# The last sixteen images' modes are turned ahead of the coefficient spread instead of behind the low modes

## The chip, the cores and the metric

One core of one Trainium2 chip runs the whole kernel. The metric is the device time of one execution in microseconds (us). The times shown are the median, lowest and highest of three runs; the profile is of one more execution.

## The reference

The input is x with 4 batches, 64 images each, 256x256 float32. Every batch is normalized in 32 groups of columns (`_gn`), and then goes through a spectral attention block. Cut to what matters:

```python
xa_n = _inorm(xa)                                   # every image by its own mean and variance
k, q = _spec_conv(xa_n, kw, (64, 64)), _spec_conv(xa_n, qw, (64, 64))   # 16 x 8 low modes
v    = _spec_conv(xa_n, vw, (256, 256))
att  = softmax(q @ k.T * sqrt(64*64)) @ v           # 64 x 64, over the images of a batch
att  = _inorm(att) + xa
mix  = _spec_conv(_inorm(att), mix_w, (256, 256), bias=mix_bias)        # 64 x 32 modes
out  = _inorm(_inorm(mix + skip)) + att
return x + out
```

`_spec_conv` is a 2D real Fourier transform, a product of each kept mode with a complex weight, and the inverse transform.

## The kernel before

All 64 images of a batch lie in SBUF at once, in X, and their half transformed modes in Y. The kernel works batch by batch, and each batch has two parts. `attend(b)` is the middle of the computation: statistics, low modes, attention among the images, mixing of all modes, and the coefficients with which each image is put together. `produce(b, more)` then makes the output images four by four (quad u), and while there is a next batch it also loads that batch's images into the places that come free, transforms them forward and sums their squares.

Each engine has a program of its own, in an order written out by hand; they meet through counting semaphores. An engine that waits holds up everything behind it in its program. The steps that matter here:

- `raw_modes(b, m, ...)` on TensorE (PE, line 404) transforms sixteen images (m of 0 to 3) along the width. `keep_raw(b, m)` on ScalarE (ACT, L608) copies them to SBUF and gives `raw_kept`.
- `turn_modes(b, m)` on PE (L418) turns the sixteen images' modes into the layout of the mixer, 8 matmuls that the trace shows as 16 records, in two groups of eight images; it gives `modes_made`. Group g (0 to 7) is then squared by ACT (`mode_powers`, L612), weighted by VectorE (DVE, `weigh_modes`, L909), and treated by GpSimd (POOL, `weigh` L833 and `add_products` L838). Groups 6 and 7 come from `turn_modes(b, 3)`.
- `energy(b, part)` on PE (L455) is a one-column matmul that sums the energies. From it DVE makes a variance (`deviations`), ACT a root (`root`, L651), and DVE the coefficients (`coefficients`, L1133 on, the last of it a memset at L1142), giving `coef_made`. Part 0 is for the first images, part 1 for the others, later in `produce`.
- `spread(b, part)` on PE (L460, L461) brings the coefficients to the partitions. `keep_spread` on DVE copies them: BIA and SCL for the images' synthesis, and C2 (L1155), from which POOL makes the factors ALPHA (`alphas`, L846; ACT adds one, L647) and scales the images X (`scale_x`, L855).
- `turn_low(b, part)` on PE (L472, 32 small matmuls, 64 records) makes the low modes' share D; DVE adds it (`add_low`, L909, Y<-Y,psB), and ACT turns the low piece (`low_piece`, L617 and L618), which gives `s_ready`.
- `inverse_h(b, q)` on PE (L433) is the inverse along the height for quad q. `keep_t` on ACT (L630) copies it, `inverse_w` on PE (L448) is the inverse along the width, `finish` on DVE (L909, X<-X,ps) adds it to the scaled image, and the sync queue stores it (L313) and loads the next batch's images in its place (L309). `forward` on PE (L386) is their forward transform.
- In the last batch ACT also writes factors for some images that DVE scales itself (`vector_alphas`, L640).

`coefficients` of part 0 works for about 2 us while `energy` has been issued and PE has nothing to do; ACT then runs `root(b, 0)`, `mode_powers(b, 5)` and `keep_raw(b, 3)` in this order.

Of the kernel before, what the change touches and what calls it, by code (L numbers as in the profile page):

```python
# [82 lines left out]
def spectral_block(nc, x, mix_re, mix_im, mix_mirror, low_w, low_mix, scalars,  # L83
# [8 lines left out]
    with ctx:  # L92
# [181 lines left out]
        def coef_bank(b, part):  # L274
            return second_bank(b) if part else psT[1]
# [20 lines left out]
        def over(ap, dims):  # L296

            return bass.AP(ap.tensor, ap.offset, [list(ap.ap[0])] + dims)
# [76 lines left out]
        def _(pe):  # L375
# [23 lines left out]
            def raw_modes(b, m, steps):  # L399

                for step in steps:
                    c, k = step // 2, step % 2
                    for t in range(2):
                        last = mm(psR[m % 2][64 * t:64 * t + 64, :], GWR[:, c, k, :, :].rearrange("p r v -> p (r v)"),  # L404
                                  Y[:, c, k, 16 * m + 8 * t:16 * m + 8 * t + 8, :],
                                  start=step == 0, stop=step == 3)
                    if step == 3:
                        last.then_inc(raw_made, 1)

            def turn_modes(b, m):  # L410

                if m:
                    pe.wait_ge(mode_weighted, 8 * b + 2 * m - 1)
                pe.wait_ge(raw_kept, 4 * b + m + 1)
                for pair in range(4):
                    for t in range(2):
                        rows = slice(64 * t, 64 * t + 64)
                        last = mm(over(psM[(2 * m + t) % 3][:, 64 * pair:64 * pair + 1], [[256, 2], [1, 64]]),  # L418
                                  raw_of(m)[rows, 128 * pair:128 * pair + 128], TURN[rows, :], start=True, stop=True)
                        if pair == 3:  # L420
                            last.then_inc(modes_made, 1)

            def inverse_h(b, q):

                for n, (q0, q1) in enumerate(PIECES):
                    if q == q0:
                        pe.wait_ge(s_ready, 3 * b + n + 1)
                if q:
                    pe.wait_ge(t_kept, 32 * b + 2 * q)
                for part in range(2):  # L430
                    for h in range(2):
                        rows = slice(64 * h, 64 * (h + 1))
                        last = mm(psT[h][:, 0:H],  # L433
                                  S[rows, q, part, :, :].rearrange("p j n -> p (j n)"),
                                  INVH[rows, part, :], start=part == 0, stop=part == 1)
                last.then_inc(t_made, 1)
# [16 lines left out]
            def energy(b, part):  # L453
                pe.wait_ge(energy_part, 10 * b + (6, 10)[part])
                mm(coef_bank(b, part)[0:IMGS, 496:497], FPH, ONES[:, 0:1],  # L455
                   start=True, stop=True).then_inc(energy_sum, 1)

            def spread(b, part):
                pe.wait_ge(coef_made, 2 * b + part + 1)
                mm(coef_bank(b, part)[:, 320:416], SIDE[:, :], RC, start=True, stop=True)  # L460
                mm(coef_bank(b, part)[:, 416:480], ONES[0:IMGS, :], E2, start=True, stop=True).then_inc(coef_spread, 1)  # L461

            def turn_low(b, part):

                j0, j1 = (0, 4 * SPLIT) if part == 0 else (4 * SPLIT, 32)
                pe.wait_ge(d_made, 2 * b + part + 1)
                for r in range(2):
                    for v in range(LV):
                        vals = D[:, r, :].rearrange("p (u v) -> p u v", v=LV)[:, :, v]
                        col = LV * r + v  # L470
                        for h in range(2):
                            last = mm(low_bank(b, part)[64 * h:64 * h + LU, col:16 * (j1 - j0):16], vals, EI[:, 2 * j0 + h:2 * j1:2],  # L472
                                      start=True, stop=True)
                last.then_inc(d_turned, 1)

            def warm(n):
                for _ in range(n):
                    mm(psZ[0][:, 0:256], ONES[:, :], FWD[:, :, :].rearrange("p a n -> p (a n)"), start=True, stop=True)

            def attend(b):  # L480

                warm(WARM[0])
                pe.wait_ge(totals_in, b + 1)
                mm(psTot[:, 0:64], ONES[:, :], TOT, start=True, stop=True).then_inc(totals_made, 1)
                for c in range(WC):
                    mm(psSta[0:IMGS, 16 * c:16 * (c + 1)], Y[:, c, 0, :, U0], GROUP[:, :], start=True, stop=True)
                pe.wait_ge(pad_made, b + 1)
                mm(psSta[0:IMGS, 32:64], PAD, SEL[:, :], start=True, stop=True).then_inc(sums_made, 1)
                warm(WARM[1])

                pe.wait_ge(scaled_w, 4 * b + 2)
                for c in range(WC):
                    for k in range(2):
                        last = mm(psZ[0][64 * k:64 * k + 64, :], GWR[:, c, k, :, :].rearrange("p r v -> p (r v)"),  # L494
                                  Y[:, c, k, :, U0 + 1:U0 + 9], start=c == 0, stop=c == WC - 1)
                last.then_inc(z_raw, 1)
                pe.wait_ge(scaled_w, 4 * b + 4)
                for c in range(WC):
                    last = mm(psZ[1][0:64, 0:IMGS], GWR[:, c, 0, :, :].rearrange("p r v -> p (r v)"),
                              Y[:, c, 0, :, U0], start=c == 0, stop=c == WC - 1)  # L500
                last.then_inc(z_raw, 1)
                raw_modes(b, 0, (0,))

                pe.wait_ge(z_kept, 2 * b + 2)
                for n in range(8):
                    mm(psZ[2][0:IMGS, 32 * n:32 * (n + 1)], ZT[:, 64 * n:64 * (n + 1)], MIRROR[:, :],
                       start=True, stop=True)
                mm(psZ[2][0:IMGS, 256:272], ZT0, MIRROR[0:64, 0:16], start=True, stop=True).then_inc(z_made, 1)
                raw_modes(b, 0, (1, 2, 3))
                raw_modes(b, 1, (0,))  # L510

                pe.wait_ge(qk_ready, b + 1)
                for n in range(8):
                    o, size = (72, 64) if n // 4 else (0, 72)
                    src = QKV[:, (n % 4) // 2, n % 2, o:o + size]
                    last = nc.tensor.transpose(psQ[0:size, 64 * n:64 * (n + 1)], src, EYE[:, :])
                last.then_inc(qk_turned, 1)
                turn_modes(b, 0)
                pe.wait_ge(qk_kept, 2 * b + 2)
                for n in range(4):  # L520
                    size, q, k = ((72, n, 2 + n), (64, 2 + n, 4 + n))[n // 2]
                    last = mm(psB[0:IMGS, 256:320], QT[0:size, q, :], QT[0:size, k, :], start=n == 0, stop=n == 3)
                last.then_inc(logits_made, 1)
                raw_modes(b, 1, (1, 2, 3))

                pe.wait_ge(probs_made, b + 1)
                nc.tensor.transpose(psB[0:IMGS, 320:384], PR[:, 0, :], EYE[:, :]).then_inc(probs_turned, 1)
                turn_modes(b, 1)
                pe.wait_ge(probs_kept, b + 1)
                mm(psA[0:IMGS, 0:2 * LOW], PR[:, 1, :], QKV[:, 2, :, :].rearrange("p r n -> p (r n)"),  # L530
                   start=True, stop=True).then_inc(att_made, 1)
                raw_modes(b, 2, (0, 1, 2, 3))
                raw_modes(b, 3, (0,))
                turn_modes(b, 2)
                raw_modes(b, 3, (1, 2, 3))
                energy(b, 0)
                spread(b, 0)
                turn_low(b, 0)
                turn_modes(b, 3)
                inverse_h(b, 0)  # L540

            def produce(b, more):
# [43 lines left out]
            for b in range(B):  # L586
                attend(b)
                produce(b, b < B - 1)
# [669 lines left out]
```

## Time and profile before

| | us |
|---|---|
| median of 3 runs (lowest to highest) | 636.29 (633.12 to 636.81) |
| profiled execution | 633.88 |
| its span in the trace | 632.1 |
| PE, DVE, ACT, POOL busy | 581.8, 482.8, 356.6, 336.4 |
| mean granted clock of PE | 0.961 |

The profiled execution is 1.8 us longer than its span, and 2.4 us shorter than the median. Times in the trace count from the span's start. A record's busy time of PE is modelled at its end, so where two records follow each other, the starts are what is read. The granted clock is a share of full speed: 1.00 is 2.4 GHz, 0.50 is 1.2 GHz.

### The profile page before, as it was taken

The page shows a single profiled execution, that of the slowest core. Times are in us where ns is not written, and L with a number is a line of the kernel's source. Part 1 is how long each engine was busy: PE and PEld are TensorE (multiplying, and loading weights), DVE is VectorE, ACT ScalarE, POOL GpSimd, SP SyncE. Part 2 cuts the span into 40 slices and gives each one's busy share as a digit, 9 for nine tenths or more (in the row PEclk, how much of TensorE's full clock was granted, in tenths as well). Part 3 has the DMA queues.
Part 4 walks back from the last instruction along what each step waited for, and adds up shares of the span by engine and source line. Part 5 has one row for each costly group of instructions (what it writes and reads, how often), then busy time and mean ns, then how long its engine had stood idle before and what let it go on. Part 6 is the DMA issues. An engine that isn't in the chain of part 4 may idle for free.

```text
span 632.1 us, 13832 instructions
## 1 busy us (share of the span) xinstructions
PE 581.8 (92%) x5072; PEld 480.6 (76%) x5072; DVE 482.8 (76%) x1095; ACT 356.6 (56%) x778; POOL 336.4 (53%) x398
## 2 busy tenths in 40 slices
PE   9999996999999996999999999699999999866994
PEld 9999644899899842789999874488999985354773
DVE  4666787787776888688777768777877768878996
ACT  6888353575666534466666635256576662543431
POOL 0270046959960014896975002597897200479993
PEclk9999996999999999899999999789999999979998
DMA  8993003899899901579999950279799993005787
GB/s 318 326 385 110 1 2 96 293 311 301 292 313 322 328 14 41 208 264 305 287 332 309 317 206 1 67 255 303 252 334 322 322 303 112 0 34 192 263 309 270
DMA packets 75522, 142.55 MB, mean 226 GB/s; under 512 B 6016, under 2 KB 6656, under 8 KB 75456
## 3 DMA queue, kind: packets, MB, share of 16 engines
q1 hardware_dynamic: 75456, 141.67, 65.6%
q8 instruction: 41, 0.67, 0.5%
q14 instruction: 25, 0.20, 0.1%
HBM read 74.54 MB, written 67.11 MB: 224 GB/s over the span
## 4 chain that ended last, share of the span: by engine, by line
PE 53%; DVE 25%; ACT 7%; POOL 5%; DMA 5%; issue 5%; SPq 0%; DVEq 0%; ACTq 0%; POOLq 0%
PE psY L386 23%; PE psP L448 15%; PE psT L433 7%; DVE QP L945 6%; DVE X L909 4%; ACT SQ L604 3%; POOL X L855 3%; DMA X<-in_x 3%; DVE Y L909 3%; DVE SQ L909 3%; DMA out<-X 2%; PE psP L494 1%; DVE IM L913 1%; DVE SQ L919 1%; DVE IM L916 1%
## 5 line engine op out<-in xcount | busy, mean ns | idle before, releaser
L855 POOL TENSOR_TENSOR X<-X,ALPHA 128x512 f32<-128x512 f32 x244 | 254.6, 1080 | 31.7 <-DVE IM L1142 18.5
L386 PE MATMUL psY<-FWD,X 128*128 128x128 f32 x1856 | 224.0, 279 | 2.3 <-DMA X<-in_x 2.2
L386 PEld LDWEIGHTS psY<-FWD,X 128*128 128x128 f32 x1856 | 213.1, 193 | 15.5 <-issue 13.9
L945 DVE TENSOR_REDUCE QP<-SQ 128x32 f32<-128x512 f32 x256 | 162.2, 680 | 48.3 <-ACT SQ L604 48.1
L909 DVE TENSOR_TENSOR X<-X,psP 128x512 f32<-128x512 f32 x192 | 125.8, 684 | 51.2 <-PE psP L448 23.9
L448 PE MATMUL psP<-INVW,T 64*128 64x256 f32 x768 | 141.9, 404 | 13.4 <-DVE X L909 7.8
L604 ACT ACTIVATE SQ<-X 128x512 f32<-128x512 f32 x232 | 132.4, 621 | 9.1 <-DVE Y L916 6.4
L833 POOL TENSOR_TENSOR Y<-Y,OMEGA 128x256 f32<-128x256 f32 x32 | 24.5, 765 | 189.0 <-ACT Y L612 189.0
L448 PEld LDWEIGHTS psP<-INVW,T 64*128 64x128 f32 x768 | 93.8, 191 | 34.2 <-ACT T L630 14.8
L630 ACT ACTIVATE T<-psT,BIA,SCL 128x256 f32<-128x256 f32 x128 | 65.3, 560 | 94.3 <-PE psT L433 89.8
L596 ACT ACTIVATE Y<-psY 128x512 f32<-128x512 f32 x128 | 76.2, 595 | 46.5 <-PE psY L386 45.3
L433 PE MATMUL psT<-INVH,Y 64*128 64x256 f32 x512 | 72.4, 402 | 0.0
L448 PE MATMUL psB<-INVW,T 64*128 64x256 f32 x256 | 68.9, 390 | 0.0
L433 PEld LDWEIGHTS psT<-INVH,Y 64*128 64x128 f32 x512 | 54.9, 203 | 5.2
L448 PEld LDWEIGHTS psB<-INVW,T 64*128 64x128 f32 x256 | 46.7, 190 | 0.0
L909 DVE TENSOR_TENSOR X<-X,psB 128x512 f32<-128x512 f32 x64 | 43.6, 682 | 1.8 <-POOL X L855 1.3
L838 POOL TENSOR_TENSOR Y<-Y 128x256 f32<-128x256 f32 x32 | 24.1, 754 | 19.7 <-DVE Y L909 19.4
L404 PE MATMUL psT<-Y,GWR 128*64 128x512 f32 x128 | 30.8, 600 | 0.0
L404 PE MATMUL psP<-Y,GWR 128*64 128x512 f32 x128 | 30.6, 598 | 0.0
L647 ACT ACTIVATE ALPHA<-ALPHA,ONES 128x256 f32<-128x256 f32 x32 | 16.2, 505 | 24.0 <-POOL ALPHA L846 24.0
L846 POOL TENSOR_TENSOR ALPHA<-MR,C 128x256 f32<-128x256 f32 x32 | 19.7, 616 | 15.0 <-DVE C L1155 11.3
L617 ACT ACTIVATE Y<-Y 128x128 f32<-128x128 f32 (+2 forms) x44 | 12.9, 293 | 23.4 <-POOL Y L838 16.6
(206 smaller groups left out, 552.5 us busy)
## 6 DMA issues: line engine op xcount, KB each, us to landing
X<-in_x SPq DMA_DIRECT2D x116, 512.0 KB, 5.4
out<-X SPq DMA_DIRECT2D x116, 512.0 KB, 3.9
X<-in_x SPq DMA_DIRECT2D x24, 256.0 KB, 4.2
Y<-in_x SPq DMA_DIRECT2D x6, 1024.0 KB, 5.1
out<-X SPq DMA_DIRECT2D x24, 256.0 KB, 3.8
INVH<-t_inv_h SPq DMA_DIRECT2D x1, 256.0 KB, 8.8
LW<-in_low_w SPq DMA_DIRECT2D x1, 204.0 KB, 5.7
FWD<-t_fwd SPq DMA_DIRECT2D x1, 128.0 KB, 2.1
```

The costliest lines, as they stand in the source:

```text
L386: last = mm(psY[p % 2][:, (2 * i + c) * 128:(2 * i + c + 1) * 128], image(nb, 2 * p + i)[:, a, c * 128:(c + 1) * 128], FWD[:, a, :], start ...
L404: last = mm(psR[m % 2][64 * t:64 * t + 64, :], GWR[:, c, k, :, :].rearrange("p r v -> p (r v)"), Y[:, c, k, 16 * m + 8 * t:16 * m + 8 * t ...
L433: last = mm(psT[h][:, 0:H], S[rows, q, part, :, :].rearrange("p j n -> p (j n)"), INVH[rows, part, :], start=part == 0, stop=part == 1)
L448: last = mm(out_bank(b, 2 * s + i)[:, W * a:W * (a + 1)], T[rows, s % 4, 128 * a:128 * (a + 1)], INVW[rows, :], start=True, stop=True)
L596: nc.scalar.activation(Y[:, :, :, i0:i0 + 3:2, :].rearrange("p c k i u -> p i (c k) u"), psY[p % 2][:, :].rearrange("p (i n u) -> p i n u" ...
L604: nc.scalar.activation(SQ[:, n % RING, :], flat_image(nb, n), ACT.Square).then_inc(squared, 1)
L630: nc.scalar.activation(T[:, p % 4, :], psT[p % 2][:, 0:H], ACT.Identity, bias=BIA[:, p:p + 1], scale=SCL[:, p:p + 1]).then_inc(t_kept, 1)
L833: P.tensor_tensor(v, v, over(OMEGA[:, 0:1], [[0, 4], [0, 2], [1, NV]]), MUL).then_inc(powers_weighted, 1)
L838: P.tensor_tensor(S[:, 2 * g:2 * g + 2, 0, :, :].rearrange("p q j n -> p q (j n)"), w[:, 0, :].rearrange("p (q n) -> p q n", q=2), w[:, 1, ...
L855: P.tensor_tensor(v, v, al, MUL).then_inc(x_scaled, 1)
L909: return V.tensor_tensor(out, a, b, op)
L945: V.tensor_reduce(QP[:, 4 * (k % 2) + place(n) % 4, :], SQ[:, n % RING, :].rearrange("p (a g j) -> p g a j", a=HC, j=GW), AX.XY, ADD).then ...
```

## The change

In `attend` of TensorE, `turn_modes(b, 3)` moves from behind `turn_low(b, 0)` to a place behind `energy(b, 0)`, ahead of `spread(b, 0)`. Nothing else is changed, on no other engine.

```diff
                 turn_modes(b, 2)
                 raw_modes(b, 3, (1, 2, 3))
                 energy(b, 0)
+                turn_modes(b, 3)
                 spread(b, 0)
                 turn_low(b, 0)
-                turn_modes(b, 3)
                 inverse_h(b, 0)
```

On TensorE, in each of the four batches, the difference of the two orders is this one, with what each row waits for; L418 is the turn, L460 and L461 the spread, L472 the low modes, L433 `inverse_h`:

```order
 L455 MATMUL psT<-ONES,Y 64x1 [waits energy_part]
+L418 MATMUL psY<-TURN,Y 128x2x64 [waits raw_kept,mode_weighted]
+L418 MATMUL psY<-TURN,Y 128x2x64 x7
 L460 MATMUL psT<-Y,SIDE 128x96 [waits coef_made]
 L461 MATMUL psT<-Y,ONES 128x64
 L472 MATMUL psB<-Y 17x20 [waits d_made]
 L472 MATMUL psB<-Y 17x20 x31
-L418 MATMUL psY<-TURN,Y 128x2x64 [waits raw_kept,mode_weighted]
-L418 MATMUL psY<-TURN,Y 128x2x64 x7
 L433 MATMUL psT<-INVH,Y 128x256 [waits s_ready]
```

The eight matmuls now stand ahead of the coefficients' spread, and `inverse_h` directly behind the low modes. On ScalarE the same stretch is the same before and now; it gives `raw_kept` (the L608 row, for which the moved step waits) and it has a group that the moved step makes (the L612 row behind the low piece):

```order
L651 ACTIVATE IM<-IM 64x1 [waits var_made]
L612 ACTIVATE Y<-psP 128x256 [waits modes_made]
L608 ACTIVATE Y<-psP 128x512 [waits raw_made]
L647 ACTIVATE ALPHA<-ALPHA,ONES 128x256 [waits alpha_made]
L617 ACTIVATE Y<-Y 128x2x2x8 [waits d_added]
L618 ACTIVATE Y<-Y 128x2x2x8
L612 ACTIVATE Y<-psY 128x256 [waits modes_made]
L630 ACTIVATE T<-psT,BIA,SCL 128x256 [waits t_made,scl_kept]
```

Nothing moved on this engine.

## Rows read from the trace of the kernel before

**Rows 1.** The page, busy us (share of the span) and instructions.
```profile
PE 581.8 (92%) x5072; PEld 480.6 (76%) x5072; DVE 482.8 (76%) x1095; ACT 356.6 (56%) x778; POOL 336.4 (53%) x398
```
**Rows 2.** Chain of waits, first batch: start us, us, what.
```profile
101.71 1.24 PE psB L472 x64
102.95 2.01 PE psY L418 x16
104.95 1.73 PE psT L433 x8
```
**Rows 3.** Timeline, first batch: start us, us, engine, line, [idle before <-releaser].
```profile
97.56 0.28 PE L455 MATMUL psT<-ONES,Y 128*64 128x1 f32 x2 [2.44 <-DVE Y L909]
98.73 0.58 ACT L608 ACTIVATE Y<-psP 128x512 f32<-128x512 f32 x1
100.59 0.74 PE L460 MATMUL psT<-Y,SIDE 64*128 64x96 f32 x2 [2.76 <-DVE IM L1142]
102.99 1.35 DVE L909 TENSOR_TENSOR Y<-Y,psB 17x64 f32<-17x64 f32 x4
103.64 0.21 ACT L618 ACTIVATE Y<-Y 128x32 f32<-128x32 f32 x1
117.94 3.84 PE L386 MATMUL psY<-FWD,Y 128*128 128x128 f32 x32
```
**Rows 4.** Chain of waits, last batch.
```profile
559.00 0.58 POOL ALPHA L846
573.74 1.28 ACT psY L640 x4
```
**Rows 5.** Timeline of TensorE, an earlier turn in the first batch.
```profile
79.73 1.11 PE L418 MATMUL psY<-TURN,Y 64*128 64x128 f32 x15
```
**Rows 6.** Windows: us, busy of PE, PEld, DVE, ACT, POOL, PEclk, DMA share, GB/s.
```profile
98.00:98.50 0.50, 0.00 (x0) 0.00 (x0) 0.46 (x3) 0.14 (x2) 0.00 (x0) 0.68 0.07 16
111.50:112.00 0.50, 0.50 (x6) 0.41 (x4) 0.00 (x0) 0.50 (x2) 0.50 (x2) 0.67 1.04 401
...
251.50:252.00 0.50, 0.00 (x0) 0.00 (x0) 0.46 (x4) 0.00 (x0) 0.07 (x1) 0.78 0.93 356
258.50:259.00 0.50, 0.10 (x2) 0.00 (x0) 0.00 (x0) 0.29 (x1) 0.50 (x1) 0.89 0.00 0
...
401.50:402.00 0.50, 0.22 (x2) 0.13 (x2) 0.21 (x1) 0.35 (x2) 0.00 (x0) 0.97 0.00 0
...
555.50:556.00 0.50, 0.00 (x0) 0.00 (x0) 0.50 (x3) 0.36 (x1) 0.50 (x1) 0.57 0.00 0
562.00:562.50 0.50, 0.50 (x6) 0.37 (x4) 0.50 (x1) 0.00 (x0) 0.50 (x1) 0.61 0.00 0
```
**Rows 7.** Timeline, last batch.
```profile
555.28 0.58 ACT L608 ACTIVATE Y<-psP 128x512 f32<-128x512 f32 x1
557.13 0.74 PE L460 MATMUL psT<-Y,SIDE 64*128 64x96 f32 x2 [2.75 <-DVE IM L1142]
```
**Rows 8.** Timeline of TensorE, second and third batch.
```profile
249.50 0.28 PE L455 MATMUL psT<-ONES,Y 128*64 128x1 f32 x2 [2.46 <-DVE Y L909]
252.53 0.74 PE L460 MATMUL psT<-Y,SIDE 64*128 64x96 f32 x2 [2.75 <-DVE IM L1142]
...
268.30 3.84 PE L386 MATMUL psY<-FWD,Y 128*128 128x128 f32 x32
...
401.44 0.28 PE L455 MATMUL psT<-ONES,Y 128*64 128x1 f32 x2 [2.44 <-DVE Y L909]
```
**Rows 9.** Chain of waits, ends of the first and second batch.
```profile
207.02 4.95 DMA X<-in_x
...
352.51 5.69 DMA out<-X
358.22 5.42 DMA X<-in_x
```
**Rows 10.** Timeline of VectorE, last batch.
```profile
573.75 0.69 DVE L909 TENSOR_TENSOR X<-X,psP 128x512 f32<-128x512 f32 x1 [1.03 <-POOL X L855]
```

## The prediction

> **What bounds the kernel now.** The page first: TensorE is busy for 92% of the span and VectorE for 76% [rows 1]. Such shares say little of a hand-over between two batches, so the second view is the chain of waits around the first hand-over. There the chain runs from VectorE (the coefficients) to TensorE: the low modes (`turn_low`), the sixteen matmul records of `turn_modes(b, 3)`, then `inverse_h(b, 0)` [rows 2]. At first sight those 2.01 us stand on the path to the first output. The third view, the timeline, shows two gaps of TensorE there [rows 3]. After the small matmul of `energy` (97.56) it idles for 2.76 us until `spread` starts at 100.59. And `inverse_h` waits for `s_ready`, which ScalarE gives when its low piece ends, at 103.64 + 0.21 = 103.85; it starts at 104.95, because TensorE is still turning modes: 1.10 us of room.
>
> The question is then who waits for what stands between. Two things hang on `spread`: TensorE's own low modes, and VectorE's `keep_spread`, which gives C2 to GpSimd, whose factors and scaling of X start with it. In the last batch the chain goes that way: GpSimd's ALPHA at 559.00 is on it, and it stays with GpSimd until ScalarE's factors at 573.74 [rows 4]. So there the start of `spread` is the path, and the start of `inverse_h` is not.
>
> **When the moved step can start.** It waits for `raw_kept` number 4, that is ScalarE's `keep_raw(b, 3)`, which stands behind `root(b, 0)` and so behind `energy`. In the first batch this ends at 98.73 + 0.58 = 99.31 [rows 3]. A wait costs some 0.04 us between an end and the next start (the chain's issue pieces), so 99.35. The other wait, for the fifth `mode_weighted`, is long over. The change cannot put the step into the earlier gap ahead of `energy`.
>
> **How long it takes.** At full clock fifteen such records took 1.11 us [rows 5]; at half clock sixteen took 2.01 us [rows 2]. Which one holds is read from the granted clock in half-microsecond windows [rows 6]: a mean of 0.68, between 1.00 ahead and 0.50 behind, puts the fall in 98.00 to 98.50 at about 98.2; likewise 251.8, 402.0 and 555.6. `keep_raw` ends 99.31 - 97.56 = 1.75 us after `energy` starts in the first batch; added to the second's and the third's `energy` (249.50 and 401.44 [rows 8]) this gives 251.3 and 403.2 there. So in the first, third and last batch (where it is 555.9, below) the fall comes before the moved step can start; it runs at 1.2 GHz and takes 2.01 us. In the second batch it has 0.5 us at 2.4 GHz.
>
> **What it does to `spread`.** First batch: 99.35 + 2.01 = 101.36, against a start of 100.59 before: 0.77 us later. Last batch: `keep_raw` ends at 555.28 + 0.58 = 555.86, the turn runs from 555.90 to 557.91, and `spread` started at 557.13 [rows 7]: 0.78 later. Second batch: about half the turn is done at full clock in 0.5 us, the other half takes 1.0, so it ends at 252.8 against 252.53, 0.25 later [rows 8]. If the clock were still full, 99.35 + 1.1 = 100.45 would be ahead of 100.59 and the step would be free. A little is won back, because `spread` no longer starts from a standstill: its four records took 100.59 to 101.71, 1.1 us, where four records inside the turn take 0.5. The gain is between 0 and 0.6; I take 0.1, since here each weight load uses the same half of the array, while in the turn two halves alternate. The Trainium skill (TensorE: Matmul & The Clock Gate, Part 1, on queue depths) says that TensorE can pull a weight load ahead of matmuls in flight; by that alone the gain would be nearer to its upper end, and the delay about 0.5 instead of 0.7. The trace doesn't show it here, since `spread`'s load had nothing in front of it.
>
> **What it does to `inverse_h`.** Everything behind `spread` (low modes, `add_low` at 102.99, ScalarE's low piece) slides by 0.77 - 0.1 = 0.67: `s_ready` at 103.85 + 0.67 + 0.04 = 104.56. `inverse_h` then starts 0.39 us earlier than at 104.95. Of the 1.10 us of room, two thirds go to the delay. ScalarE's `mode_powers(b, 6)`, which used to wait for the turn and stands ahead of the first `keep_t`, no longer waits; it fits into the time of `inverse_h`, so it is counted at nothing. If `inverse_h` ran ahead of it, it would cost 0.4.
>
> **What a start is worth in the first three batches.** The trace has its own experiment. In the second batch the clock came back at about 258.6, 7 us after it fell, in the first at about 111.8, 14 us after. So the first forward transform of the next batch starts 268.30 - 249.50 = 18.80 us after `energy` in the second batch and 117.94 - 97.56 = 20.38 in the first [rows 3, 8]: TensorE is 1.58 us ahead. The last load of the batch lands at 207.02 + 4.95 - 97.56 = 114.41 and at 358.22 + 5.42 - 249.50 = 114.14: 0.27 ahead [rows 9]. And the next `energy` comes 249.50 - 97.56 = 151.94 and 401.44 - 249.50 = 151.94 us later: nothing is left [rows 3, 8]. The store of 352.51 took 5.69 us in the second, so an earlier TensorE meets a longer DMA queue. A microsecond at the start is thus worth 0 to 0.17 at the end. For three batches, with a shift between -0.4 (TensorE) and +0.8 (GpSimd), that is -0.2 to +0.4 in sum; without the cushion, -1.2 to +2.4. I take 0.
>
> **Last batch.** No load follows. GpSimd starts 0.78 - 0.1 = 0.68 later and is on the chain until 573. VectorE waited for it: 1.03 us ahead of the piece at 573.75 [rows 10]. ScalarE's factors follow, then the second coefficients, and VectorE paces the rest to the end. I take the 0.68 in full (0 if the chain has another branch close by).
>
> **Sum.** 0 + 0.7 against this execution: 633.88 becomes 634.6. The median of the runs is 636.29, 2.4 above that execution, so the forecast is 636.3 + 0.7 = 637.0. The runs themselves lie between 633.1 and 636.8; a difference under 1% can hardly be told from none here.
>
> **Rivals.**
> 1. *The room is cashed* (faster): each of the first three batches gives the whole 1.10 us to the end and the last batch loses nothing, 636.3 - 3.3 = 633.0. For it: the turn stands on the chain [rows 2]. Against it: the half clock, which makes the turn longer than what is left of the gap, and the two equal 151.94. Chance 0.12.
> 2. *The clock stays up* (faster): TensorE's idle time ahead of `spread` is cut by work from 99.35 on; if the clock then doesn't fall, the turn is free, `spread` takes half (0.55 off the last batch), and TensorE wins about 5 us of its 14 at half clock in each hand-over, at 0.17 of worth 0.85, three times: 636.3 - 0.55 - 2.6 = 633.1. Against it: in three of four batches the fall comes before the moved step can begin [rows 6]. The Trainium skill (TensorE: Matmul & The Clock Gate, Part 1) says that half clock is the default and that activity releases it; by that rule alone work in the idle stretch should help. Chance 0.1.
> 3. *The clock comes back later* (slower): now turn and `inverse_h` make one unbroken stretch, 102.95 to 106.7. In the second and the last batch the clock rose at 258.6 and 562.4, right behind such a stretch [rows 6]. The change parts the two: the turn goes ahead, and a gap of some 0.8 us comes before `inverse_h`. If the rise slips by 7 us there as in the first batch, TensorE loses half of it, up to 3.4 us. With 0.17 of worth that is 0.6 in the second batch, but 3.4 in the last, where nothing cushions it: 637.0 + 0.6 + 3.4 = 641.0. It decides only where TensorE's lag in the last batch outgrows what VectorE waits for GpSimd anyway (about 1 us at 573 [rows 10]). Chance 0.18. The Trainium skill (TensorE: Matmul & The Clock Gate, Part 1) ties full clock to sustained activity; the rises in the trace, right behind unbroken stretches, agree.
> 4. *The change does nothing*: the order shows that the step moves, but GpSimd's 0.7 could vanish in other slack: 636.3. It is inside my forecast, which has a chance of 0.6.
>
> **Numbers.** The forecast's own range is 635.5 to 638.5 by the terms; with the rivals on either side and the scatter of single runs, 633.0 to 640.5, which leaves out the far part of rival 3 and what lies below rivals 1 and 2. Faster by over 1% means under 629.9, which no case gives: 0.02. Slower by over 1% means over 642.7, the worst of rival 3 with no cushion anywhere: 0.04. The rest, 0.94, is within 1%.
>
> **What would show it.** In the changed profile: the records of the turn start about 1.8 us after `energy`, at half clock 2.0 us long; `spread` starts without idle time behind them, 3.6 to 3.8 us after `energy` instead of 3.03; `inverse_h` starts 7.0 us after `energy` instead of 7.39, now with a wait for ScalarE; GpSimd's first ALPHA in the last batch comes 5.6 us after `energy` instead of 4.89; the distance from `energy` to `energy` stays near 152. I am wrong if the clock no longer falls, if that distance shrinks by a microsecond, or if in the last batch VectorE waits for TensorE where it waited for GpSimd.

## The result, and the profile after

| | before | changed |
|---|---|---|
| median of 15 runs, us | 635.60 | 638.28 |
| lowest to highest | 632.75 to 637.04 | 635.11 to 640.76 |
| profiled execution | 633.88 | 640.76 |
| span of its trace | 632.1 | 639.0 |
| mean granted clock of it | 0.961 | 0.948 |

The ratio, taken of the means, is 1.0047, interval 1.0028 to 1.0065: about 3.0 us slower (1.8 to 4.1), where I had forecast 0.7. The profiled execution of the changed kernel is its slowest one, and 3.2 us of its distance to the one of before lie ahead of any changed instruction (`energy` of the first batch starts at 100.76 against 97.56), so all that follows is read from `energy` on.

The timeline of the changed kernel in the first batch, where [rows 3] showed the one before:

```profile
100.76 0.28 PE L455 MATMUL psT<-ONES,Y 128*64 128x1 f32 x2 [2.44 <-DVE Y L909]
...
101.93 0.58 ACT L608 ACTIVATE Y<-psP 128x512 f32<-128x512 f32 x1
...
102.65 2.08 PE L418 MATMUL psY<-TURN,Y 64*128 64x128 f32 x16 [1.62 <-ACT Y L608]
...
104.49 0.58 PE L460 MATMUL psT<-Y,SIDE 64*128 64x96 f32 x2
...
105.37 1.32 PE L472 MATMUL psB<-Y 64*17 64x20 f32 x64
106.19 0.61 POOL L846 TENSOR_TENSOR ALPHA<-MR,C 128x256 f32<-128x256 f32 x1 [3.37 <-DVE C L1155]
...
107.64 2.08 PE L433 MATMUL psT<-INVH,Y 64*128 64x256 f32 x8 [0.95 <-ACT Y L618]
```

The turn starts 1.89 us after `energy` (forecast 1.79) and the spread stands right behind it, at 3.73 instead of 3.03. GpSimd's first ALPHA comes at 5.43 instead of 4.90, 0.53 later (in the last batch before, 559.00 in [rows 4] less the `energy` at 554.11). `inverse_h` comes at 6.88 and waits 0.95 for ScalarE; before, its first record in the same view began at 7.18. All of this is the same within 0.01 us in all four batches of this execution, also in the second, where I had expected a cheaper turn: this time the clock had fallen ahead of it (1.30 us after `energy`, against 2.28 before). In another execution of the changed kernel (below, "changed, again") it fell 2.21 us after the second batch's `energy`, inside the turn, and there the cheaper turn shows: the spread starts 3.43 us after `energy` instead of 3.73.

```profile
250.42 0.28 PE L455 MATMUL psT<-ONES,Y 128*64 128x1 f32 x2 [2.45 <-DVE Y L909]
252.31 1.82 PE L418 MATMUL psY<-TURN,Y 64*128 64x128 f32 x16 [1.62 <-ACT Y L608]
253.85 0.58 PE L460 MATMUL psT<-Y,SIDE 64*128 64x96 f32 x2
```

The windows of the changed kernel around the falls and rises of the clock (columns as in [rows 6]):

```profile
100.50:101.00 0.50, 0.24 (x2) 0.19 (x2) 0.20 (x1) 0.35 (x2) 0.12 (x1) 0.91 0.00 0
114.50:115.00 0.50, 0.50 (x8) 0.45 (x6) 0.00 (x0) 0.50 (x2) 0.50 (x2) 0.94 1.04 406
254.50:255.00 0.50, 0.00 (x0) 0.00 (x0) 0.50 (x3) 0.46 (x1) 0.44 (x1) 0.51 0.50 160
268.00:268.50 0.50, 0.50 (x6) 0.39 (x6) 0.06 (x1) 0.00 (x0) 0.50 (x2) 0.84 1.05 402
408.00:408.50 0.50, 0.34 (x2) 0.37 (x4) 0.46 (x2) 0.02 (x1) 0.34 (x1) 0.61 0.55 115
421.50:422.00 0.50, 0.50 (x6) 0.39 (x6) 0.45 (x1) 0.00 (x0) 0.50 (x1) 0.74 1.08 418
561.50:562.00 0.50, 0.02 (x2) 0.05 (x2) 0.50 (x3) 0.34 (x1) 0.50 (x1) 0.71 0.00 0
575.00:575.50 0.50, 0.50 (x6) 0.41 (x4) 0.14 (x1) 0.02 (x1) 0.50 (x2) 0.64 0.00 0
```

From the means (as in the prediction) the clock is down from 100.9 to 114.6, 254.5 to 268.2, 408.1 to 421.8 and 561.7 to 575.4: 13.7 us in every batch. Before, it was 13.7, 6.8, 13.7 and 6.8 [rows 6]. The distance from one `energy` to the next grew from 151.94, 151.94 and 152.67 to 152.45, 153.06 and 153.82, and the last piece (from the last batch's `energy` to the end) from 77.99 to 78.91: 0.51 + 1.12 + 1.15 + 0.92 = 3.7 us for this pair of executions.

The mean granted clock is known of every run. Twice its distance from 1, times the span, is the **time at half clock**. In the 15 runs of the changed kernel it is 57 to 66 us, 63.2 on average. In 29 runs of the kernel before, from the first series below and on another chip, it is 33 to 57, 45.6 on average. So the profiled pair was no accident of one execution.

The down time alone does not say when the clock is back. In the profiles of the kernel before and of "turn twice" below, which also keeps turn and `inverse_h` together, the clock fell 0.2 to 0.7 us after `energy` in four batches and was down 13.7 us each time; in the other four it fell 1.4 to 2.4 us after and was down 6.8. In the changed kernel it fell between 1.3 and 1.9 us after `energy` in four of the eight batches of its two profiles, and was down 13.7 in all four. What sets the moment of the fall, no run here shows.

### The profile page after: what moved, and what is told of

Same layout as the page of the kernel before. It is cut to its first block and busy times, and to the rows that moved or that the text cites. A ratio compares the mean times of both kernels' runs of the same rounds, so it can differ in the third digit from the quotient of the medians.

```text
span 639.0 us, 13832 instructions
## 1 busy us (share of the span) xinstructions
PE 588.3 (92%) x5072; PEld 485.7 (76%) x5072; DVE 482.3 (75%) x1095; ACT 356.0 (56%) x778; POOL 336.5 (53%) x398
## 5 line engine op out<-in xcount | busy, mean ns | idle before, releaser
L448 PE MATMUL psP<-INVW,T 64*128 64x256 f32 x768 | 146.0, 414 | 11.0 <-DVE X L909 6.5
L448 PEld LDWEIGHTS psP<-INVW,T 64*128 64x128 f32 x768 | 96.9, 198 | 33.0 <-ACT T L630 12.1
L433 PE MATMUL psT<-INVH,Y 64*128 64x256 f32 x512 | 74.9, 414 | 3.8 <-ACT Y L618 3.8
L448 PE MATMUL psB<-INVW,T 64*128 64x256 f32 x256 | 70.9, 399 | 0.0
L433 PEld LDWEIGHTS psT<-INVH,Y 64*128 64x128 f32 x512 | 55.6, 207 | 10.3 <-ACT Y L618 4.3
L448 PEld LDWEIGHTS psB<-INVW,T 64*128 64x128 f32 x256 | 48.0, 195 | 0.0
L418 PE MATMUL psY<-TURN,Y 64*128 64x128 f32 x192 | 22.4, 334 | 6.5 <-ACT Y L608 6.5
```

Source lines behind the costliest of these rows:

```text
L433: last = mm(psT[h][:, 0:H], S[rows, q, part, :, :].rearrange("p j n -> p (j n)"), INVH[rows, part, :], start=part == 0, stop=part == 1)
L448: last = mm(out_bank(b, 2 * s + i)[:, W * a:W * (a + 1)], T[rows, s % 4, 128 * a:128 * (a + 1)], INVW[rows, :], start=True, stop=True)
```

## The experiments

Two theories stood against each other. Theory A: the spread is late, and so, through C2, are GpSimd and the queue of transfers. Theory B: `turn_modes(b, 3)` and `inverse_h` no longer make one stretch without idle time, and the clock comes back later. Two series of four kernels and one of three were run, each on one chip with its own runs of before. In the table, the number of runs, the ratio with its interval, the time at half clock (mean over the runs) and, from each kernel's one profile, when spread, ALPHA, `inverse_h` and the next batch's first forward start after `energy` (first batch).

| kernel | runs | ratio to before | half clock | spread | ALPHA | inverse_h | forward |
|---|---|---|---|---|---|---|---|
| before (three series) | 29, 25, 17 | 1 | 45.6, 44.3, 45.3 | 3.03 | 4.90 | 7.18 | 20.38 |
| changed | 15 | 1.0047 (1.0028 to 1.0065) | 63.2 | 3.73 | 5.43 | 6.88 | 20.08 |
| turn twice | 12 | 1.001 (0.999 to 1.003) | 47.7 | 3.74 | 5.44 | 7.72 | 18.92 |
| bridge | 12 | 1.0046 (1.0023 to 1.007) | 56.9 | 3.73 | 5.44 | 7.00 | 20.21 |
| split | 12 | 0.9998 (0.998 to 1.0016) | 49.1 | 3.03 | 4.90 | 6.34 | 18.37 |
| filled, changed order | 6 | 0.9935 (0.9915 to 0.9955) | 25.8 | 3.03 | 4.44 | 5.89 | 17.91 |
| gap | 6 | 1.0081 (1.0052 to 1.011) | 60.3 | 3.03 | 4.89 | 7.84 | 21.45 |
| changed, again | 12 | 1.0039 (1.0015 to 1.0063) | 58.9 | 3.73 | 5.44 | 6.89 | 20.66 |
| filled, old order | 8 | 0.9938 (0.9914 to 0.9962) | 8.5 | 3.03 | 4.44 | 5.89 | 17.91 |
| filled everywhere | 12 | 0.9942 (0.9919 to 0.9964) | 10.5 | 3.04 | 4.44 | 5.90 | 17.91 |
| filled, spread late | 12 | 1.0031 (1.0009 to 1.0053) | 9.9 | 4.28 | 5.69 | 7.14 | 19.15 |
| filled, with gap | 6 | 0.9936 (0.9915 to 0.9957) | 7.5 | 3.03 | 4.44 | 6.46 | 17.91 |
| filled, old order, again | 6 | 0.9938 (0.9914 to 0.9961) | 9.8 | 3.04 | 4.45 | 5.90 | 17.90 |

**Turn twice.** The late spread without the parting.

```diff
                 energy(b, 0)
+                turn_modes(b, 3, told=False)   # the same matmuls, no signal
                 spread(b, 0)
                 turn_low(b, 0)
                 turn_modes(b, 3)
                 inverse_h(b, 0)
```

> The order before, but the eight matmuls of the turn run twice: once ahead of the spread (without a signal) and once in their old place. So the spread is held up as in the change (about 0.5 us at half clock), and the turn still stands right ahead of inverse_h. Theory A (the late spread costs, through GpSimd and the queue of transfers behind it): as slow as the change or slower, 2 to 3.5 us over before, near 638; GpSimd's first ALPHA 5.4 us after the energy matmul instead of 4.9. Theory B (the change costs because the turn and inverse_h are parted, and the clock comes back later): the clock rises as before, in some batches 7 us after it fell, and the time is within 1 us of before, 636.

The timeline of TensorE in the first batch of this kernel:

```profile
99.38 2.08 PE L418 MATMUL psY<-TURN,Y 64*128 64x128 f32 x16 [1.62 <-ACT Y L609]
101.22 0.58 PE L460 MATMUL psT<-Y,SIDE 64*128 64x96 f32 x2
...
102.10 1.31 PE L472 MATMUL psB<-Y 64*17 64x20 f32 x64
103.34 2.08 PE L418 MATMUL psY<-TURN,Y 64*128 64x128 f32 x16
105.20 1.28 PE L433 MATMUL psT<-INVH,Y 64*128 64x256 f32 x8
```

ALPHA is as late as in the change (5.44) and `inverse_h` later still, but the ratio is 1.001: on average over the runs 1.1 us over before (635.06 against 633.98), of which the interval does not exclude 0. The clock comes back as before, 47.7 us at half clock. Read against the change's 3.0, most of the loss is not the late spread's. Theory A alone falls; a late spread as a part of the loss does not.

**Bridge.** The changed order with the gap ahead of `inverse_h` filled.

```diff
                 turn_low(b, 0)
+                for _ in range(2):
+                    mm(psZ[0][:, 0:128], ONES[:, :], FWD[:, 0, :], start=True, stop=True)
                 inverse_h(b, 0)
```

> The changed order with two idle matmuls of 128 columns between the low modes and inverse_h, so that the gap of 0.95 us there is filled. Theory A: as slow as the change, 638, since the spread is as late. Theory B: the clock comes back earlier in some batches (7 instead of 14 us after the fall) and most of the loss is gone, 636.

The timeline of TensorE, first batch:

```profile
102.67 1.31 PE L472 MATMUL psB<-Y 64*17 64x20 f32 x64
103.91 1.22 PE L541 MATMUL psP<-FWD,ONES 128*128 128x128 f32 x4
105.06 2.08 PE L433 MATMUL psT<-INVH,Y 64*128 64x256 f32 x8
```

The gap is filled, and the kernel is as slow as the change. Against expectation by theory B the clock came back late in all four batches of the profile, and over the runs half clock fell only from 63.2 to 56.9 us (the change's second set of runs has 58.9). From 103.91 to the end of `inverse_h` the filled stretch lasts 2.9 us, where turn and `inverse_h` together lasted 3.7 [rows 2]. Counted with the turn, the spread and the low modes, TensorE worked here without idle time for over 7 us, from 1.89 after `energy` to the end of `inverse_h`; before, it did so for some 6, from 3.03 on. So a stretch without idle time is not by itself what brings the clock back, and the run does not tell the theories apart.

**Split.** Half of the turn on either side.

```diff
                 energy(b, 0)
-                turn_modes(b, 3)
+                turn_modes(b, 3, (0, 1))      # pairs 0 and 1
                 spread(b, 0)
                 turn_low(b, 0)
+                turn_modes(b, 3, (2, 3))
                 inverse_h(b, 0)
```

> Half of the turn (its pairs 0 and 1, about 1.0 us at half clock) ahead of the spread, the other half behind the low modes. The first half ends before the coefficients are there, so the spread starts 3.03 us after the energy matmul as before; inverse_h starts about 1.0 us earlier than before. Theory A: nothing is lost, 635 to 636, perhaps 0.3 better than before. Theory B: the unbroken stretch ahead of the first wait for ScalarE is 1 us shorter, so the clock still comes back late in some batches, 636.5 to 638.

Spread and ALPHA are as early as before, `inverse_h` 0.84 earlier, and the time is that of before (633.91 against 633.98 on average), with 49.1 us at half clock. This fits theory A's number; of the late clock that theory B feared, the half clock time shows little (3.5 us more than before). It also shows that 0.84 us of `inverse_h` alone buys nothing that can be measured.

**Gap.** The order before, turn and `inverse_h` parted by one wait, spread untouched.

```diff
                 turn_modes(b, 3)
+                pe.wait_ge(powers, 8 * b + SPLIT + 2)
                 inverse_h(b, 0)
```

> The order before, with one more wait ahead of inverse_h: for ScalarE's square of the turn's first group (seventh of the batch), which ends about 0.4 us behind the turn. The spread is as early as before, the turn in its old place, but the turn and inverse_h no longer touch. Theory B (the clock comes back later when that stretch is parted): the time at half clock grows from about 46 us of an execution towards the 63 of the change, and the kernel is 1.5 to 3 us slower than before. Theory A (the late spread costs): no loss beyond the 0.45 us by which inverse_h starts later, at the worth of a start 0 to 0.3 us.

The timeline of TensorE, first batch, and the windows of 22 us that hold each hand-over (columns as in [rows 6]):

```profile
103.00 2.08 PE L418 MATMUL psY<-TURN,Y 64*128 64x128 f32 x16
105.55 2.08 PE L433 MATMUL psT<-INVH,Y 64*128 64x256 f32 x8 [0.47 <-ACT Y L613]
...
119.16 3.84 PE L386 MATMUL psY<-FWD,Y 128*128 128x128 f32 x32
```

```profile
97.50:119.50 22.00, 17.78 (x169) 14.33 (x170) 14.52 (x39) 8.60 (x25) 17.55 (x22) 0.69 0.51 182
249.50:271.50 22.00, 16.12 (x156) 13.00 (x158) 14.48 (x40) 7.51 (x22) 16.54 (x20) 0.69 0.42 153
402.00:424.00 22.00, 15.55 (x150) 11.85 (x148) 14.52 (x39) 7.91 (x24) 16.39 (x21) 0.69 0.37 134
555.00:577.00 22.00, 15.13 (x144) 10.98 (x140) 14.77 (x41) 7.54 (x25) 15.37 (x19) 0.69 0.07 25
```

A pause of 0.47 us, with ALPHA as early as before, makes the kernel 0.8% slower, some 5 us. The clock's mean is 0.69 in every one of the four windows: 0.31 x 2 x 22 = 13.7 us at half clock, each time, though it fell 1.5 to 1.9 us after `energy`, where before and turn twice, after such falls, had it back after 6.8. This is theory B without theory A's late spread, and larger than forecast (1.5 to 3 us). It is not the longer down time alone, though. From one `energy` to the next, and to the end, this profile is 1.72, 1.73, 1.27 and 0.8 us longer than the one of before, and in the first and third batch the clock was down 13.7 us in both. There it fell, and so rose, 1.3 us later after `energy`, and `inverse_h` stood 0.66 later. Both can weigh on these two batches, and the run does not part them.

**Changed, again.**

> The changed kernel once more, as a control on the chip of this series: 1.003 to 1.006 of before, about 63 us of every execution at half clock, no execution under 55.

1.0039, so the effect holds on another chip; half clock was 54 to 64 us, 58.9 on average: less than the 63 expected, and my floor of 55 was a little high. In its profile the clock was down 13.7 us in three batches and 10.2 in the second.

**Filled, changed order and old order.** Idle matmuls of 256 columns, whose result nobody reads, keep TensorE at work around `energy`. `warm(n)` issues n of them; the kernel before already has six in each batch, further ahead.

```diff
+                warm(4)
                 energy(b, 0)
+                warm(3)                # old order: warm(5), and no turn here
                 turn_modes(b, 3)
                 spread(b, 0)
```

> The changed order, with four idle matmuls of 256 columns ahead of the energy matmul and three behind it, in TensorE's idle time. If that keeps the clock at 2.4 GHz, the turn takes 1.1 us and no longer holds up the spread, and the spread itself takes half. Theory A: GpSimd starts 0.5 us earlier than before and 1.0 earlier than in the change, four times: 633 to 634.5. Theory B: no fall of the clock at all, TensorE has up to 5 us less work at each hand-over: 632 to 634.5. If the clock falls all the same: 638 or more.

> The order before, with four idle matmuls of 256 columns ahead of the energy matmul and five behind it: the clock is held up without the change. Theory B: what counts is the time at half clock, so it is as fast as the filled version of the changed order, 0.990 to 0.996 of before; with the clock up the two orders differ by under 1 us, the changed one being ahead, since its turn is free there and inverse_h starts up to 1 us earlier.

The old order filled, first batch, the timeline of TensorE and the same kind of windows:

```profile
97.71 0.28 PE L455 MATMUL psT<-ONES,Y 128*64 128x1 f32 x2 [0.52 <-DVE Y L911]
97.91 2.43 PE L478 MATMUL psP<-FWD,ONES 128*128 128x256 f32 x10
100.74 0.46 PE L460 MATMUL psT<-Y,SIDE 64*128 64x96 f32 x2 [0.40 <-DVE IM L1144]
...
101.32 1.27 PE L472 MATMUL psB<-Y 64*17 64x20 f32 x64
102.52 1.16 PE L418 MATMUL psY<-TURN,Y 64*128 64x128 f32 x16
103.60 1.13 PE L433 MATMUL psT<-INVH,Y 64*128 64x256 f32 x8
```

```profile
97.50:119.50 22.00, 19.29 (x210) 16.23 (x211) 15.34 (x40) 11.61 (x32) 18.01 (x22) 1.00 0.56 192
249.50:271.50 22.00, 19.49 (x212) 16.41 (x214) 15.35 (x39) 11.71 (x32) 18.27 (x21) 1.00 0.59 198
402.00:424.00 22.00, 19.49 (x218) 16.29 (x216) 15.56 (x36) 11.06 (x28) 19.49 (x23) 1.00 0.62 211
555.00:577.00 22.00, 13.63 (x144) 10.74 (x138) 17.16 (x34) 10.81 (x32) 21.79 (x24) 1.00 0.32 120
```

The clock does not fall in any of the four windows, the turn takes 1.16 us instead of 2.08, and both orders are 0.6% faster than before (0.9935 and 0.9938). In both, spread, ALPHA and `inverse_h` start at the same time (3.03, 4.44, 5.89). In the changed order the clock still fell for 3.4 us in three of the four batches of the profile.

**Filled everywhere.**

```diff
                 turn_low(b, 0)
+                warm(2)
                 inverse_h(b, 0)
+                warm(1)
```

> The filled version of the changed order with idle matmuls in the two later gaps as well: two of 256 columns ahead of inverse_h, one behind it. In the filled version the clock still fell for 3.4 us in three of four batches, about 7.5 us behind energy. If these gaps are the cause, it doesn't fall here; less than 15 us at half clock, and 0.990 to 0.994 of before. If an idle matmul delays inverse_h, up to 0.3 us per batch is lost.

The short falls of the filled changed order are gone (10.5 instead of 25.8 us), and it buys nothing more: 0.9942. The filled old order, which has no such gap, needs no such matmuls. This is also the fair comparison of the two orders with the clock up, both in one series: 0.9942 for the changed one, 0.9938 for the old. What the change costs, late spread included, it costs only where the clock falls.

**Filled, spread late,** the old order with `warm(9)` in place of `warm(5)`; **filled, with gap,** the old order with the wait of the gap experiment; and the control.

> The order before with the clock held up, but nine idle matmuls behind energy instead of five, so that the spread is late by some 1.7 us in every batch while the clock stays at 2.4 GHz. This prices a late spread by itself. If it costs in the last batch alone, 1.5 to 2 us over the filled old order; if GpSimd's start passes through in every batch, 5 to 7 us; if it has slack everywhere, under 0.5.

> The order before with the clock held up, and the added wait of the gap experiment ahead of inverse_h. Theory B (what the gap cost was the clock): the gap costs nothing here, within 1 us of the filled old order, and half clock stays under 15 us. If the gap itself costs, it is 3 to 5 us slower than the filled old order, as it was without the filling.

> The filled old order once more, as the control of this series: 0.992 to 0.996 of before, under 15 us at half clock.

The kernel with the late spread, TensorE, first batch:

```profile
98.00 0.28 PE L455 MATMUL psT<-ONES,Y 128*64 128x1 f32 x2 [0.53 <-DVE Y L911]
98.20 4.15 PE L478 MATMUL psP<-FWD,ONES 128*128 128x256 f32 x18
102.28 0.46 PE L460 MATMUL psT<-Y,SIDE 64*128 64x96 f32 x2
```

Spread, ALPHA, `inverse_h` and forward are all late by 1.24 to 1.25 us (less than the 1.7 I had reckoned with), the clock stays up, and the median is 635.8 against 629.9: 5.9 us for four delays of 1.25, which are 5.0. By the intervals of the two ratios the 5.9 can be 4 to 8. So at full clock a hand-over that is late as a whole, GpSimd and TensorE alike, is paid about in full over the execution; this is not the price of GpSimd's start alone. Which batches pay is open: against the mean of the three other filled kernels of the old order, this kernel's profile (its fastest run) is longer by 0.5, 2.1, 1.1 and 0.2 us, while those three differ among themselves by up to 1.5 in one batch. The kernel with the gap, on the contrary, costs nothing (629.92 against 629.91):

```profile
102.64 1.16 PE L418 MATMUL psY<-TURN,Y 64*128 64x128 f32 x16
104.27 1.13 PE L433 MATMUL psT<-INVH,Y 64*128 64x256 f32 x8 [0.47 <-ACT Y L615]
```

Its pause is the same 0.47 us, `inverse_h` is 0.57 later, and forward starts at 17.91 as without it. So the pause costs its 5 us only together with the half clock; at full clock it has slack.

## Why the prediction was right or wrong

**Right: sign and range.** Slower, within 1%; 638.28 lies inside the stated range, which was wide enough for most of rival 3. That it also lies inside the forecast's own 635.5 to 638.5 is luck: the median of before came out 0.7 us lower this time (635.60 for 636.29), and as a difference that range was -0.8 to +2.2. The size was wrong: 0.7 us forecast, 3.0 measured.

**Right: the steps at the hand-over.** The turn behind `keep_raw`, at half clock and 2.1 us long; the spread 0.70 late against 0.77, the turn starting 0.10 later than reckoned and taking 1.84 to the next start; `inverse_h` earlier by 0.30 against 0.39; its new wait for ScalarE. What the spread wins back behind a running TensorE was put at 0.1: it was some 0.2, so GpSimd's start slid by 0.53 and not by 0.68. Of the signs named, these came true, and VectorE still waits for GpSimd in the last batch (longest wait 2.1 us, 1.0 before); the distance of 152 did not hold.

**Open: the last batch.** 0.7 was forecast, and the pair of profiles has 0.92. The path is as forecast: in the second profile of the changed kernel the chain of waits goes from the turn over the spread to GpSimd (start us, us, what; last batch).

```profile
557.44 2.08 PE psY L418 x16
559.51 0.34 PE psT L460 x2
...
560.98 0.58 POOL ALPHA L846
...
562.88 2.06 POOL X L855 x2
```

The size isn't shown. The last piece of that profile, and those of turn twice and bridge, all with ALPHA some 0.5 us later, are 0.1, 0.6 and 0.9 us shorter than the one of before; the gap's is 0.8 longer with ALPHA on time, and there the chain goes over TensorE's low modes, turn and `inverse_h`. Over the thirteen profiles a straight-line fit gives 1.1 us per us of ALPHA with a standard error of 0.5, and 0.1 per us of `inverse_h` with one of 0.7. The agreement of 0.92 with 0.7 can be luck.

**Wrong: the worth of a start in the first three batches,** put at 0 to 0.17, so that the term was 0. It was read from one pair of batches, in which only TensorE's forward was earlier while ALPHA stood at 4.90 in both. That showed what an earlier TensorE is worth while GpSimd's start is fixed, not what a later start of either costs. And two equal distances of 151.94 were too little to build on: the same filled kernel, run twice, has 150.03 in one profile's third batch and 151.54 in the other's. A hand-over late as a whole costs, at full clock, 1.2 us per us (5.9 for 5.0). A fit over the 39 distances from `energy` to `energy` of the thirteen profiles gives 0.60 us per us of forward and 0.45 per us of ALPHA (standard errors 0.09 and 0.23), with 0.46 us of scatter. The first batch of the changed profile points the same way (the same 13.7 us at half clock, forward 0.30 earlier, ALPHA 0.53 later, the distance 0.51 longer), but one such difference is no larger than the scatter.

**Wrong: rival 3 was given 0.18 and belonged in the sum.** That the clock comes back later when the two are parted, and that this costs time, the gap experiment with its filled twin shows: with turn and `inverse_h` in one stretch the clock was back after 7 us in some batches; parted, it takes 14 us nearly always. The reason that I gave for it, the unbroken stretch, is not enough: before, all four batches had the same stretch, and in two of them the clock stayed down; in the bridge, with a longer one, it stayed down in all four. Its price was put in the wrong place: I expected little in the second batch and 3.4 us in the last. In the profiles the second batch lost 1.12, and the last 0.92 with GpSimd's delay in it. The two parts are not independent enough to split the 3.0 exactly. Turn twice (late spread, clock nearly as before) puts the spread's part between -0.6 and 1.9 us by its interval; what is left, some 2 us, goes with the 15 to 18 us more at half clock. Both parts hang on the half clock: at 2.4 GHz the turn takes 1.16 us and no longer holds up the spread.

**Rival 1** (the room is cashed) falls: the split gave `inverse_h` 0.84 us earlier at an unchanged spread, and 0.9998. **Rival 2** (the clock stays up): not by the change, whose work begins too late in the idle stretch, but with idle matmuls in all of it the forecast price of 3.2 us was near: 3.5 to 4.6 measured, by the medians of the series.

**Open.** Why the bridge brought back so little of the full clock while the split kept it; longer bridges were not run. And the scatter of single runs, 1.3 to 1.7 us, goes only partly with the clock (correlation 0.39, 0.50 and 0.77 in the three series of the kernel before); the rest isn't explained.

## What to carry to other kernels

Moving matmuls into an idle stretch can cost more than it saves: before taking work away ahead of a dense stretch, look in the windows whether the clock comes back right behind it, and count in several executions how long the clock is down. Where TensorE idles at a hand-over, a few idle matmuls that end before the next real one is released can pay: they gained 0.6% here, while the change of order alone lost 0.4 to 0.5%; four more of them, which held up the spread, cost 5.9 us. A worth read from one pair of stretches holds only for what differed in them; price a delay by a run that makes it, at a fixed clock, and over many executions: single stretches of one kernel differ here by up to 1.5 us.

## What the runs showed that I had not expected

A pause of 0.47 us between two blocks of matmuls, in each of four batches, cost 5 us of 634 where the clock falls and nothing where it stays up. Where the clock fell in a hand-over, it was down for 3.4, 6.8, 10.2 or 13.7 us in all profiles, and in the changed kernel's two profiles for 13.7 in seven batches of eight. And 36 added idle matmuls in an execution made the kernel 4.5 us faster, their own price, if any, included.
